# A transformer block with routed experts on one core: expert tables made in two parts and sent through DRAM, eight buffers of expert rows

## The reference

```python
h = layernorm(x) * (1 + ca) + sa
x = x + ga * attn_ref(h, ...)       # 16 heads of 8, relative bias, causal, then an MLP of 512
h = layernorm(x) * (1 + cb) + sb
x = x + gb * ffn_ref(h, ...)

def ffn_ref(x, ...):                # E = 32 experts, K = 4, I = 96
    scores = sigmoid(x @ gate_w.T)
    _, ids = top_k(scores + e_bias, 4)
    w = take_along_axis(scores, ids); w = w / sum(w)
    a = silu(x @ w1[e]) * (x @ w3[e])      # only a token's four experts weigh
    return sum over the four of  w * (a @ w2[e])
```

## Time and profile before

| | |
|---|---|
| device time, median of 3 runs | 630.68 us (629.22 to 632.84) |
| profiled execution, first to last instruction (its span; no other time of it is given) | 628.9 us |
| mean granted clock of TensorE, 1 = 2.4 GHz | 0.911 |
| busy TensorE / VectorE / ScalarE / GpSimd | 490.9 / 449.7 / 337.4 / 387.8 us |
| DMA moved | 73.40 MB, mean 117 GB/s |

### The profile page before, as it was taken

One profiled execution on the slowest core, in us unless ns is written; L12 is line 12 of the kernel. 1 busy time (PEld: TensorE's weight loads), 2 busy tenths in 40 slices (PEclk: granted clock), 3 DMA queues, 4 the chain that ended last, 5 costly groups with the idle time before them and its releaser, 6 DMA issues.

```text
span 628.9 us, 16754 instructions
## 1 busy us (share of the span) xinstructions
PE 490.9 (78%) x4648; PEld 387.1 (62%) x4649; DVE 449.7 (72%) x1487; ACT 337.4 (54%) x756; POOL 387.8 (62%) x620
## 2 busy tenths in 40 slices
PE   2457989999999887677778573068898999999677
PEld 0234666666666656566666452048887999899556
DVE  5777888888888874765998958624565666666637
ACT  1236888788878885345555433126555665444200
POOL 5465666666666530154677777777777777777610
PEclk8568999999999999899989795559999999999779
DMA  6999400000005104211111115356666445544198
GB/s 202 274 294 272 122 0 1 0 0 0 0 1 213 58 3 126 81 47 39 54 62 58 57 61 155 111 151 179 171 174 162 134 135 145 138 131 125 47 381 303
DMA packets 82167, 73.40 MB, mean 117 GB/s; under 512 B 9936, under 2 KB 73648, under 8 KB 82112
## 3 DMA queue, kind: packets, MB, share of 16 engines
q1 hardware_dynamic: 65408, 50.72, 28.7%
q0 software_dynamic: 8192, 17.84, 7.7%
q10 hardware_dynamic: 8512, 4.20, 2.2%
HBM read 43.22 MB, written 32.65 MB: 121 GB/s over the span
## 4 chain that ended last, share of the span: by engine, by line
PE 29%; DVE 26%; issue 19%; POOL 6%; DVEq 6%; SPq 6%; DMA 4%; ACT 4%; POOLq 0%; ACTq 0%
DVE L L1408 7%; PE PS L1017 6%; POOL xs L685 5%; DVE yidx L1796 3%; PE PS L1040 3%; SPq L449 3%; PE PS L1137 3%; PE PS L992 3%; PE PS L1125 3%; PE PS L1329 2%; DVEq L343 2%; PE PS L1020 2%; PE PS L1056 2%; DVE YQ L1794 2%; SPq L434 2%
## 5 line engine op out<-in xcount | busy, mean ns | idle before, releaser
L685 POOL DMA_INDIRECT xs<-YQ,posi x128 | 123.9, 968 | 77.3 <-issue 65.0
L703 POOL DMA_INDIRECT ys<-YQ,yidx x128 | 122.6, 958 | 40.9 <-issue 34.5
L1408 DVE TENSOR_TENSOR L<-PS,BIAS 128x768 f32<-128x768 f32 x128 | 116.6, 952 | 24.3 <-PE PS L1020 21.6
L751 ACT ACTIVATE PR<-L 128x768 f32<-128x768 f32 x128 | 105.9, 842 | 44.1 <-DVE L L1408 36.7
L1794 DVE SCALAR_TENSOR_TENSOR YQ<-PS,tag,YQ 128x128 f32 x192 | 67.4, 351 | 58.6 <-DVE yidx L1796 34.4
L1260 PE MATMUL PS<-BIAS,V 128*128 x384 | 75.7, 341 | 3.3 <-issue 1.1
L1260 PEld LDWEIGHTS PS<-BIAS,V 128*128 128x128 f32 x384 | 62.3, 192 | 11.9 <-issue 11.9
L1017 PE MATMUL PS<-YQ 32*128 32x256 f32 x512 | 46.9, 436 | 17.4 <-DVE L L1408 16.0
L899 ACT ACTIVATE L<-PS 128x384 f32<-128x384 f32 x48 | 23.6, 491 | 67.7 <-PE PS L1260 64.5
L1137 PE MATMUL PS<-w2s,hid 128*128 128x128 f32 x256 | 34.0, 288 | 14.2 <-ACT hid L821 14.2
L1017 PEld LDWEIGHTS PS<-YQ 32*128 32x128 f32 x512 | 20.9, 188 | 36.6 <-DVE L L1408 19.7
(11 more groups left out here) (278 smaller groups left out, 1129.4 us busy)
## 6 DMA issues: line engine op xcount, KB each, us to landing
PR<-xs SPq DMA_DIRECT2D x192, 72.0 KB
BIAS<-ys SPq DMA_DIRECT2D x12, 512.0 KB, 8.0
xs<-pad_row SPq DMA_DIRECT2D x65, 72.0 KB, 21.2
xs<-pad_row SPq DMA_DIRECT2D x1, 4608.0 KB, 26.7
modb<-mod_rows SPq DMA_DIRECT2D x1, 4096.0 KB, 13.6
dist_rep<-dist_row SPq DMA_DIRECT2D x4, 768.0 KB, 8.2
X<-in_x ACTq DMA_DIRECT2D x4, 512.0 KB, 6.1
BIAS<-dist_rep SPq DMA_DIRECT2D x4, 512.0 KB, 8.3
```

The source lines that it names most:

```text
L685: pool.indirect_dma_start(out=xs, out_offset=bass.IndirectOffsetOnAxis(ap=posi[j][:, t * TOPK + k:t * TOPK + k + 1], axis=0), in_=ROWS[j][ ...
L703: pool.indirect_dma_start(out=ys, out_offset=bass.IndirectOffsetOnAxis(ap=yidx[:, n:n + 1], axis=0), in_=YQ[:, n * D:(n + 1) * D], in_offs ...
L751: act.activation(PR[u % 4][:, :], L[u % 2][:, :], ACT.Exp).then_inc(s["exp_done"], 1)
L1408: return dve.tensor_tensor(L[u % 2][:, :].rearrange("p (j w) -> p j w", j=2), PS[:, at:at + 2, 0:HW], BIAS[:, u, :].rearrange("p (j w) -> ...
```

## The change

- `modb` becomes two gate arrays, `gates[0]` (ga) and `gates[1]` (gb), loaded by two DMAs of 512-byte pieces (2048 KB each, replicated); `moda` keeps a place of its own. The load stands behind the pad writes at the start and waits only for `md_pe`. sb and cb are no longer loaded.
- There are `BUFS` = 8 buffers of expert rows: four where they were, three over `moda`, one over hT and LM, which now lie in one array `early`. ScalarE's wait for scatters goes back eight batches. H2T moves from PR to YNT and YN. ScalarE clears LM once after attention.
- A table is made for each part, 32 columns wide. Part 0's (128 passes, 32 steps) is made by VectorE after `place(13)`, part 1's (64 passes, 16 steps) inside steps 1 and 2 of the loop. TensorE has no part in it: SyncE writes the integers to a DRAM array `table`, transposed, and loads them back to `treg`. SyncE, GpSimd, TensorE and VectorE wait for `ld_t` = 16 (part 0) or 48 (part 1).
- The loop therefore needs only part 0's table to begin. The loops of PE and DVE are cut where part 1 begins; GpSimd's `y_rows` is unrolled.

```diff
+BUFS = 8
+PTILES = [FIRST_PART * TPB * TOPK + NE, (NB - FIRST_PART) * TPB * TOPK + NE]
...
-            sp.wait_ge(s["h_ready"], NB)
-            sp.dma_start(modb[:, :, :, :].rearrange("p b m d -> p b (m d)"),
-                         bass.AP(mod_rows.tensor, 2 * D, [[0, P], [6 * D, NB], [1, 4 * D]])).then_inc(s["ld_mod"], 16)
+            sp.wait_ge(s["md_pe"], 1)
+            for i in range(2):
+                sp.dma_start(gates[i], bass.AP(mod_rows.tensor, (2 + 3 * i) * D, [[0, P], [6 * D, NB], [1, D]])
+                             ).then_inc(s["ld_mod"], 16)
...
-            sp.wait_ge(s["t_ready"], 1)
+            def table_out(part):
+
+                sp.wait_ge(s["t_ready"], part + 1)
+                sp.dma_start(table[part].rearrange("j p -> p j"), tv[:, part, :], allow_slow_non_contiguous=True).then_inc(s["wr_t"], 16)
+
+            def table_in(part):
+
+                sp.wait_ge(s["wr_t"], 16 * (part + 1))
+                n = 3 if part else 4
+                sp.dma_start(treg[0:1, part:part + 2 * n - 1:2, :], table[part:part + 1, 0:n, :]).then_inc(s["ld_t"], 16)
+                if part:
+                    g = slice(PGROUPS, SLOTS * LIVES // YGROUP)
+                    sp.dma_start(treg[0:1, 6, g], table[part:part + 1, 3, g]).then_inc(s["ld_t"], 16)
+            table_out(0)
+            table_in(0)
+            sp.wait_ge(s["ld_t"], 16)
...
+            early_fours = PTILES[0] // (4 * XG) - 1
+            for i in range(early_fours):
+                if NE + 8 * i < NV:
+                    zero_behind(NE + 8 * i)
                 load_four(4 * i)
+                if i == early_fours - 3:
+                    table_out(1)
+                if i == early_fours - 2:
+                    table_in(1)
...
                 act.wait_ge(s["r_lg"], b + 1)
-                if not at(b, 0, 1, 2, 3):
-                    act.wait_ge(s[f"scat{n}"], used * (16 * TPB * TOPK))
+                if b >= BUFS:
+                    act.wait_ge(s[f"scat{b % BUFS}"], scattered(b % BUFS, b))
...
             yn_T(NB - 1)
+            act.activation(LM, zero[:, :].to_broadcast([P, UW]), ACT.Copy)
             m_evac(1, 1)
...
             pe.wait_ge(s["h2_copies"], NB)
-            for j in range(4):
-                last = pe.matmul(PS[0:1, 1, j * P:(j + 1) * P], tv[:, j:j + 1], ident[:, :], start=True, stop=True)
-            last.then_inc(s["tv_pe"], 1)
-            pe.wait_ge(s["tv_ready"], 2)
-            for j in range(3):
-                last = pe.matmul(PS[0:1, 0, j * P:(j + 1) * P], tv[:, 4 + j:5 + j], ident[:, :], start=True, stop=True)
-            last.then_inc(s["tw_pe"], 1)
-            pe.wait_ge(s["t_ready"], 1)
-            pe.wait_ge(s["tw_ready"], 1)
+            pe.wait_ge(s["ld_t"], 16)
...
                 if places:
                     pick(*places[1])
                     place(*places[1])
+                    if places[0][0] == FIRST_PART:
+                        counted(0)
+                        table_ends()
+                        table_rows(0)
...
             for i in range(4):
                 step(i, i)
-            with dve.Fori(1, XSTEPS // 4 - 1) as four:
+                if i == 1:
+                    table_ends()
+                if i == 2:
+                    table_rows(1)
+            with dve.Fori(1, PTILES[0] // (4 * XG)) as four:
+                for n in range(4):
+                    step(four * 4 + n, n)
+            dve.wait_ge(s["ld_t"], 48)
+            with dve.Fori(PTILES[0] // (4 * XG), XSTEPS // 4 - 1) as four:
                 for n in range(4):
                     step(four * 4 + n, n)
```

More of the change, by code:

```diff
@@ L143, in build @@
         XH = sb("XH", [P, TPB, D])
-        hT = [sb(f"hT{i}", [P, SEQ]) for i in range(2)]
+        early = sb("early", [P, 2 * SEQ + UW])
+        hT = [early[:, i * SEQ:(i + 1) * SEQ] for i in range(2)]
         HB = [sb(f"HB{i}", [P, TPB, D]) for i in range(2)]
@@ L274, in build, with scattered @@
         pairs = [pair_of(2 * k, 2 * (k % 2)) for k in range(NPAIR)]
+        def scattered(n, batches=NB):
+            return 16 * TPB * TOPK * len([b for b in range(batches) if b % BUFS == n])
         def part_of(b):
@@ L464, in _ @@
             sp.wait_ge(s["pad_ready"], 2)
[L465 to L469, removed]
-                load_four(4 * i)
-            for i in range(GROUP):
-                sp.wait_ge(s[f"scat{i}"], 16 * NT * TOPK // GROUP)
+            early_fours = PTILES[0] // (4 * XG) - 1
+            for i in range(early_fours):
+                if NE + 8 * i < NV:
+                    zero_behind(NE + 8 * i)
+                load_four(4 * i)
+                if i == early_fours - 3:
+                    table_out(1)
+                if i == early_fours - 2:
+                    table_in(1)
+            for i in range(BUFS):
+                sp.wait_ge(s[f"scat{i}"], scattered(i))
             sp.wait_ge(s["pad_done"], 16 * NV)
-            with sp.Fori(early, XSTEPS // 4 - 1) as four:
+            sp.wait_ge(s["ld_t"], 48)
+            with sp.Fori(early_fours, XSTEPS // 4 - 1) as four:
                 load_four(four * 4)
@@ L705, in y_rows @@
                                 in_=YQ[:, n * D:(n + 1) * D], in_offset=None).then_inc(s[f"yst{n // 16}"], 16)
-            pool.wait_ge(s["tw_ready"], 1)
+            pool.wait_ge(s["ld_t"], 16)
             passes_of = treg[0:1, 6, :]
-            with pool.Fori(0, LIVES) as life:
+            for life in range(LIVES):
                 y_rows(life)
@@ L875, in turn @@
                 for i, batch in enumerate(rows):
-                    scored(*batch, used)
+                    scored(*batch)
                     copies(*batch, ROW_BANKS[i])
@@ L1187, in ranks, with turn @@
                 count(2 * half + 1, tri, OH[n % 2][:, 1, :, :]).then_inc(s["r_rank"], 1)
-            def turn(products, rows, places, nxt, k, used):
+            def turn(products, rows, places, nxt, k):
                 if products:
@@ L1679, in place, with counted, table_ends @@
                                              ALU.mult, ALU.add).then_inc(s["pad_ready"], 1)
-            def turn(products, rows, places, nxt, k, used):
+            def counted(p):
+                st(dve.tensor_copy(cnt[:, :], bank(6, NE, p * TPB * NE)))
+            def table_ends():
+                st.wait()
+                st(dve.tensor_tensor_scan(ends[:, :], onesf[:, :], cnt[:, :], 0.0, ALU.mult, ALU.add))
+                st.wait()
+                for j in range(2):
+                    last = dve.tensor_scalar(endi[:, j, :], ends[:, :], float(j * (P - 1)), None, ALU.add)
+                st(last)
+                st.wait()
+                st(dve.tensor_scalar(endi[:, :, :], endi[:, :, :], 7, None, ALU.logical_shift_right))
+                st.wait()
+                st(dve.tensor_copy(edge[:, :, :], endi[:, :, :]))
+                st.wait()
+                st(dve.tensor_tensor(part[:, :], edge[:, 1, :], edge[:, 0, :], ALU.subtract))
+                st.wait()
+                st(dve.tensor_tensor_scan(upto[:, :], onesf[:, :], part[:, :], 0.0, ALU.mult, ALU.add))
+                st(dve.scalar_tensor_tensor(lead[:, :], part[:, :], float(-P), cnt[:, :], ALU.mult, ALU.subtract))
+                st.wait()
+                st(dve.tensor_tensor(tend[:, :], edge[:, 0, :], upto[:, :], ALU.add))
+                st(dve.tensor_scalar(lead[:, :], lead[:, :], float(REGION), None, ALU.add))
```

211 lines of the change are left out of this document (99 added, 112 removed).

## The result

The changed kernel takes 639.84 us (median of four runs, 634.07 to 641.33) beside 631.45 us (629.22 to 632.84) for the kernel before on the same chip: ratio 1.0129, 95% interval 1.0093 to 1.0164. The prediction, 630.3 us with a range to 634.0, was wrong. The profiled execution took 640.58 us, its span 638.6, against 628.9 before: 9.7 us more. Ratios marked * come from two later sets of runs in which the kernel before took 809.45 and 807.28 us (medians), and of those sets only ratios, attention and the table's first write are used.

The account below looks back on a forecast made before the run. Bound taken: GpSimd's scatter chain to its 64th result scatter, then 20 loop steps, then the gather. Span 628.9 - 0.2 + 0 = 628.7; adding back 1.8 gives 630.5, forecast 630.3 us, range 625 to 634.

Parts of the forecast that it names:

- the early start: Expert loop would start some 12 us earlier, silu(0) at 410 instead of 422.11; all but 0.99 us lost at later waits.
- I take 5 plus 2 for reading back: 400: First table's DMAs: transposed write 5 us, reading back 2, done at 400; bounds 397 and 406.
- place(12): VectorE's batch 12 before the first table, done at 377.76 in the kernel before, would come about 5 us earlier.
- Its DMAs have four steps to land: Second table, made in loop steps 1 and 2: its DMAs have four steps to land; no cost summed.
- rival 2: Slower: TensorE's clock at half rate after clear(28)'s wait, steps 27 to 30; mostly 632 to 635 us, chance 0.16.
- clear(24) and clear(28): ScalarE's loop waits for result scatters to free slots: 6.5 us at the first, 5 to 6.5 at the second.
- ScalarE's four waits for row scatters: In the last batches, 19.0 us together; would go because eight row buffers let batch b wait for b - 8.
- Edits (a) and (b): Gate vectors loaded early, and ScalarE's extra clearing of LM: each cost 0, at most 2 us and 0.9.
- The table's instructions: First table on VectorE, some 30 instructions: 6.5 us, ready at 390.5.
- what comes after the gate: Behind clear(28): VectorE without arrears, TensorE at a slow clock; net -0.2 us, ends -1.2 and +1.4.
- edit (c): Second table's 30 VectorE instructions in steps 1 and 2: perhaps 6 us late, covered by waits; uncovered, 6 us.
- the forecast 628.7: Span of the changed kernel: 628.9 - 0.2 + 0 = 628.7 us.

Follow-up runs that it names:

- copy16: Changed kernel, tables written as 16-byte pieces, reordered by a VectorE copy, second table sent earlier: ratios 1.0021 and 1.0143; third time (copy16_c) 630.98 us, ratio 0.9998.
- before_write: Kernel before plus one transposed write of 512 4-byte pieces that nobody reads, behind the fifth group of row loads: 637.54 us, ratio 1.0126.
- bufs4_c: Changed kernel with four row buffers instead of eight, third time: 643.36 us, ratio 1.0185; the two earlier times gave ratios 1.0073 and 1.0113.
- twice: Changed kernel with the second table written a second time, to a place nobody reads, right behind the first writing: 636.59 us, ratio 1.0124.
- write_early: Changed kernel with the second table's write three groups of row loads earlier: 636.02 us, ratio 1.0103.
- before_attn_b: Kernel before plus the transposed write of 512 words in the middle of attention, second time: ratio 1.002; the first time (before_attn) gave 1.0119.
- attn_64: Kernel before plus 512 words of 4 bytes written in mid-attention, 64 bytes apart in DRAM: one run, 630.59 us, first row scatter at 264.17.
- attn_twice: Kernel before plus two writes of 512 words side by side, one behind the other in attention: one run, 637.01 us, first row scatter at 268.85.
- attn_spread: Kernel before plus 512 words of 4 bytes written in mid-attention, 512 bytes apart in DRAM: one run, 629.7 us, first row scatter at 264.06.
- attn_16: Kernel before plus 128 pieces of 16 bytes written side by side in mid-attention: one run, 630.82 us, first row scatter at 264.80.

## Why the prediction was wrong

The step that failed is the table's transposed write, twice: once in the sum and once beside it. Only the second made the kernel slower. The first ate the early start, which copy16 shows to be worth nothing by itself.

- As a term of the sum. "I take 5 plus 2 for reading back: 400" was 10.86 plus 2.31. The prediction allowed for 10 and still had a start at 405. It was 413.25, since SyncE was free at 398.28, not 393 (place(12) came 1.2 us earlier, not 5; the pads took 20.47, not 19.78), and 1.8 us of register loads stand between read and row loads: 5.3 + 5.9 + 0.3 + 1.8 = 13.3 us over the 400. The nearest row that I chose, 128 single words loaded in 6.5 us, was a read, and says nothing of words written side by side.
- As a cost beside the path. "Its DMAs have four steps to land" priced the second write by when its data is wanted. It landed in time and cost 10.0 us all the same (in this execution; 2.9 in the traced one of before_write, the fastest of its four), by stopping ScalarE and VectorE on its way. No rival had this; rival 2 had a slow TensorE clock, but as the child of a wait at clear(28) that never came. The clock added only 2.5 of the 10 us.

Right, and shown by copy16 once the write is cheap: the start 10 us earlier, waits of 5.16 and 6.54 us at clear(24) and clear(28) (forecast 6.5 and 5 to 6.5), silu(28) at 521.46 (520.98), result scatters from 439.04, no net gain. ScalarE's four waits for row scatters, 19.0 us together, are gone as forecast; in bufs4_c there are four again, 18.4 us. Edits (a) and (b) and whatever else touches attention, priced at 0, make its end 0.9 us later in the mean: first row scatter 264.67 to 265.81 in the ten traces with the change, 263.77 to 264.80 in the seven without it and without a pause. The table's instructions took 5.0 us (388.14 to 393.1) for the 6.5 I took, ready 2.5 us late because batch 12 was.

Mis-sized there: -0.2 us for what comes after the gate. The product of silu(30) was at 530.75 in copy16_c, 1.0 later than before, since the granted clock stayed at 0.50 to 524 and averaged 0.69 to 528. The Trainium skill ("TensorE: Matmul & The Clock Gate", HAM oscillation) says that such a loop pays the return to full speed at each long wait. The rows agree: the step behind clear(24) and the one behind clear(28) took 4.64 us each, where 3.36 is usual.

The range was also narrower than it says: it claims both bounds of every cost, but rival 2 reaches 635 and the uncovered 6 us of edit (c) would reach 636.5.

That copy16_c's span is the forecast 628.7 to the tenth is luck: its first gather came 1.0 us later than before, and what follows the gather took 1.2 us less, neither of which was in the sum.

The first write's time also varies. In the profiled executions of twice and write_early the first write went out at 394.91 and 393.95 with the same code, 3 to 4 us ahead of the 398.28 above, and their loops began 3.3 and 3.7 us ahead of the kernel before. So the early start is not always eaten whole by the first write, and part of the spread from 634 to 641 us may come from there; the second write's pause then eats more than it.

The Trainium skill ("DMA: Bandwidth & Descriptors", Specifications) says of transfers under 512 B that "below this, SDMA does read-modify-write". No run here shows such a step. What the runs show is that small size alone is not the price: words side by side took 10.86 us and stopped engines, words 64 and 512 bytes apart, as small, landed in 3.1 and 2.3 us and held nobody up. The measurement decides: what to look at is which pieces lie close together.

Open: what the engines wait for. By the traces' records of single packets, other transfers were slow behind the write too. In the changed kernel 24 packets that started within 14 us of 494.31 took over 1 us each, the longest, pieces of row loads, up to 3.42; the rest of the loop from 425 to 600 has 6 of them, and copy16_c none within 14 us of its second write. Code comes by DMA as well, in queues that the profile calls "instruction", and one of its packets was slow: in before_attn_b the only one from 106 to 111 us took 3.91 us, the longest such packet of all 20 traces. At the same place it took 1.30 in attn_64 and 0.95 in the kernel before (the lines below, of these three in that order: packets, MB, share of the 16 engines' time from 106 to 111).

```profile
q8 instruction: 1, 0.02, 4.9%
q8 instruction: 1, 0.02, 1.6%
q8 instruction: 1, 0.02, 1.2%
```

That is one packet. Code that comes late would explain a pause of engines whose inputs are ready. Against it as the whole answer: before_attn and attn_twice have the pause and no packet of these queues from the write to its end, the changed kernel has none between 484.00 and 512.50, and GpSimd, whose result scatters are unrolled code, went on. That late code is what stops the engines is argued, not shown.

## What to carry to other kernels

Do not transpose through DRAM word by word: let each partition write its few bytes as one piece, and reorder on an engine, or keep the pieces 64 bytes apart (measured in attention only, once). A DMA whose result is wanted late is not free for that: ask what else it can stop, and try it alone in the old kernel, as before_write did for 1.3%. When a start moves forward, look for the next gate (here slots freed by GpSimd's chain) before counting the gain; to gain here, that chain would have to get shorter.

## What the runs showed of the hardware

- 512 words of 4 bytes side by side in DRAM: 10.7 to 11.4 us from issue to landing (six first writes), and ScalarE or VectorE still for 3.6 to 10.1 us, from 3.7 to 6.3 us after the issue on, even with DMA engines at a share of 0.00. 64 bytes apart (attn_64): landed in 3.1 us, no pause.
- 128 pieces of 16 bytes side by side (2 KB too): 1.4 to 3.2 us, no pause. Two writes of 512 words, issued 0.4 and 0.5 us apart, give one pause.
- Other packets are slow behind the dense write: 24 over 1 us within 14 us in the changed kernel, none in copy16_c; a packet of code took 3.91 us in before_attn_b, 0.95 to 2.10 at the same place in before, attn_64, attn_spread and attn_16.
- Register loads with a stride of four words in SBUF, in place of neighbours, came with pauses of TensorE of up to 5.0 us at each round of its loop, 24.1 us in all. The cause is not known; in copy16_c, with contiguous loads, they are gone (1.0 us).
